# A copy moved to VectorE, four step orders, and the last feed-forward batches in banks of their own

## The reference, cut to what matters

```python
x = x + tanh(g_xattn[1]) * _L1_xattn_ref(_layernorm(x), ctx, ...)   # 16 heads of 16 channels, clipped scores
x = x + tanh(g_ffn[1])   * _L1_ffn_ref(_layernorm(x), ...)          # 16 heads, keys and values of one picked head
x = x + tanh(g_xattn[2]) * _L2_xattn_ref(_layernorm(x), ctx, ...)   # 16 heads of 128, 4 key heads, rotary, + context
x = x + tanh(g_ffn[2])   * _L2_ffn_ref(_layernorm(x), ...)          # 8-bit rows, ternary weights, hidden 1024
```

## Time and profile before

| | us |
|---|---|
| median of 3 runs | 2429.48 (2425.93 to 2430.18) |
| the profiled execution, own time | 2448.54 |
| its span, first to last instruction | 2446.4 |
| PE (TensorE matmuls) busy | 2169.1 (89%) |
| DVE (VectorE) busy | 1510.5 (62%) |
| ACT (ScalarE) busy | 1123.7 (46%) |
| POOL busy | 743.5 (30%) |

### The profile page before, as it was taken

One profiled execution on the slowest core, in us unless ns is written; L12 is line 12 of the kernel. 1 busy time (PEld: TensorE's weight loads), 2 busy tenths in 40 slices (PEclk: granted clock), 3 DMA queues, 4 the chain that ended last, 5 costly groups with the idle time before them and its releaser, 6 DMA issues. The chain is left out here.

```text
span 2446.4 us, 38415 instructions
## 1 busy us (share of the span) xinstructions
PE 2169.1 (89%) x10486; PEld 1377.7 (56%) x10486; DVE 1510.5 (62%) x3702; ACT 1123.7 (46%) x3555; POOL 743.5 (30%) x932
## 2 busy tenths in 40 slices
PE   6969999978799789978999999999998598979999
PEld 3446777855455344445555566566655355545685
DVE  6975434435566577765577677776776588843234
ACT  2022234411355355545555555556554288832242
POOL 5705510045333300013344444444443200003104
PEclk9969999989999899999999999999999599979999
DMA  6902245452400000000000000000000000201143
GB/s 217 310 17 84 92 131 162 155 156 81 172 1 0 3 1 0 0 26 1 1 1 1 0 0 0 0 0 0 0 0 1 4 6 5 107 3 46 63 136 97
DMA packets 85587, 127.18 MB, mean 52 GB/s; under 512 B 12418, under 2 KB 74626, under 8 KB 84226
## 3 DMA queue, kind: packets, MB, share of 16 engines
q1 hardware_dynamic: 75490, 98.52, 12.5%
q0 software_dynamic: 9984, 27.28, 3.5%
HBM read 91.41 MB, written 47.84 MB: 57 GB/s over the span
## 5 line engine op out<-in xcount | busy, mean ns | idle before, releaser
L2375 ACT ACTIVATE l2x_prob<-l2x_pS,l2x_nb,l2x_rms_q 128x256 f32<-128x256 f32 x256 | 142.5, 565 | 116.6 <-DVE l2x_nb L2610 114.8
L1035 ACT ACTIVATE moe_act_g<-moe_pG 128x96 f32<-128x96 f32 (+1 forms) x159 | 53.2, 335 | 279.3 <-PE moe_pU L968 119.8
L1186 PE MATMUL l2x_pQ<-big,l2x_xT 128*128 128x512 f32 x312 | 149.6, 602 | 4.8 <-DVE l2x_part L2588 4.3
L2607 DVE TENSOR_REDUCE l2x_negmax<-l2x_pS 128x2 f32<-128x512 f32 x128 | 87.8, 686 | 92.3 <-PE l2x_pS L2195 89.5
L928 POOL DMA_INDIRECT moe_yk<-route_y,moe_slot_i x72 | 69.6, 966 | 236.7 <-DMA route_y<-moe_y 187.5
L3117 DVE TENSOR_TENSOR l3f_hid<-l3f_act_g,l3f_pA 128x256 f32<-128x256 f32 (+1 forms) x103 | 38.1, 370 | 163.2 <-ACT l3f_act_g L3028 106.4
L2205 PE MATMUL l2x_pOT<-l2x_probT,l2x_v 128*128 128x512 f32 x256 | 124.7, 610 | 4.5 <-ACT l2x_probT L2390 4.5
L2195 PE MATMUL l2x_pS<-l2x_kT,l2x_qT 128*128 128x256 f32 x512 | 128.3, 380 | 0.0
L2941 PE MATMUL l3f_pA<-big,l3f_xnT 128*128 128x512 f32 x256 | 125.4, 614 | 0.0
L2214 PE MATMUL l2x_pT<-big,l2x_oT 128*128 128x256 f32 x512 | 121.1, 379 | 0.7 <-ACT l2x_oT L2383 0.7
L3028 ACT ACTIVATE l3f_act_g<-l3f_pA 128x256 f32<-128x256 f32 (+1 forms) x103 | 35.3, 343 | 183.4 <-PE l3f_pA L2941 183.4
(11 more groups left out here) (499 smaller groups left out, 5812.8 us busy)
## 6 DMA issues: line engine op xcount, KB each, us to landing
route_x<-in_c_zero SPq DMA_DIRECT2D x1, 13184.0 KB, 80.4
moe_xg<-route_x SPq DMA_DIRECT2D x103, 128.0 KB, 2.1
route_y<-moe_y SPq DMA_DIRECT2D x103, 128.0 KB, 1.7
big<-in_e_gu SPq DMA_DIRECT2D x1, 6144.0 KB, 19.2
l3f_xg<-route_x SPq DMA_DIRECT2D x39, 128.0 KB, 2.2
route_y<-l3f_y SPq DMA_DIRECT2D x39, 128.0 KB, 1.7
big<-in_f_gu SPq DMA_DIRECT2D x1, 4096.0 KB, 12.3
big<-in_e_down SPq DMA_DIRECT2D x1, 3072.0 KB, 25.2
```

What stands on the lines that cost most here:

```text
L1186: last = pe.matmul(out, lhsT=xT[:, k, :], rhs=w[:, k, cols], start=(k == 0), stop=(k == KC - 1))
L2375: ins = act.activation(prob[g % 2][:, h, :], pS[j][:, (h % 2) * 2 * P:(h % 2 + 1) * 2 * P], ACT.Exp, scale=rms_q[g][:, h:h + 1], bias=nb[: ...
L2607: dve.tensor_reduce(negmax[:, c], pS[j][:].rearrange("p (h k) -> p h k", h=2), AX.X, ALU.max, negate=True).then_inc(S["max_steps"], 1)
```

## The change

In `l1x` the whole copy of the turned keys is made by VectorE (`vector_whole`), the strips stay on ScalarE (`scalar_first`, `scalar_rest`). The step `turn` comes ahead of `normalise` and `zed`; `xT` moves behind `S3`, and `V2` ahead of `attT`, on TensorE and VectorE; ScalarE has `xT`, `attT`, `S3`. In `l1f` VectorE copies P2 ahead of the ternary step and the division, and ScalarE gets an order of its own, with P0's copy ahead of S1's exponential. In the rotary stage both `value_rows` move: for the batch's own rows into its slot 0, for the context into slot 1, each behind that slot's first `proj`. In slot 3 the output projection is cut in two halves of two heads, with the second transposes of probabilities between them. After the last slot `finish()` is written out by hand on each engine: batch 14's four projections go to `pQ`, `pTq`, `pS0`, `pS1`, and so do batch 15's, whose transposed row goes to `pP`; the hidden row of 14 is turned in `pOT`; batch 15 has a set of buffers of its own, laid over probabilities and queries that are no longer needed; the rounding of the hidden rows of 14 and 15 goes from POOL to ScalarE. The third narrow-head stage (`l3x`) is left as it is.

```diff
+    def vector_whole(self, dve, b, p):
+        dve.wait_ge(self.turned_ps, b + 1)
+        whole = self.ps_q[:, 0:4 * P] if self.spread == "k" else self.ps_k[:, 0:self.kt * P]
+        dve.tensor_copy(self.plain[p][:].rearrange("p m t -> p (m t)"), whole).then_inc(self.whole_read, 1)
+
+    def scalar_first(self, act, b, p):
+        act.wait_ge(self.turned_ps, b + 1)
+        if isinstance(b, int) and b == 0:
+            act.wait_ge(self.blank, 2)
+        parts = self.ps_k[:, 0:self.kt * P] if self.spread == "k" else self.ps_q[:, 0:4 * P]
+        self.strip(act, p, parts, 0)
+        self.strip(act, p, parts, 1)
...
-                      ("S1", 2), ("v", 1), ("V0", 2), ("rows", 1), ("S2", 2), ("normalise", 0), ("zed", 4),
-                      ("turn", 1), ("back", 3), ("divide", 3), ("V1", 2), ("spread", 1), ("xT", 0))
-        order = first_half + (("S3", 2), ("attT", 3), ("V2", 2))
-        act_order = first_half + (("attT", 3), ("S3", 2))
+                      ("S1", 2), ("v", 1), ("V0", 2), ("rows", 1), ("S2", 2), ("turn", 1), ("normalise", 0),
+                      ("zed", 4), ("back", 3), ("divide", 3), ("V1", 2), ("spread", 1))
+        order = first_half + (("S3", 2), ("xT", 0), ("V2", 2), ("attT", 3))
+        act_order = first_half + (("xT", 0), ("attT", 3), ("S3", 2))
...
+                after(pe, tq.whole_read, b)
+                    pe.wait_ge(tq.whole_read, b + 1)
...
-            steps = {"xT": lambda b, p: nm.scalar(act, b, p), "turn": lambda b, p: tq.scalar(act, b, p),
+            steps = {"xT": lambda b, p: nm.scalar(act, b, p), "turn": lambda b, p: tq.scalar_first(act, b, p),
-            pipeline(dve, order, steps, peel=6)
+            pipeline(dve, order, {**steps, "turn": lambda b, p: tq.vector_whole(dve, b, p)}, peel=6)
...
-        order = first_half + (("turn", 1), ("normalise", 0), ("S3", 2), ("ternary", 1), ("P2", 2), ("xT", 0),
-                              ("divide", 3))
+        order = first_half + (("normalise", 0), ("S3", 2), ("P2", 2), ("ternary", 1), ("divide", 3))
+        act_order = (("S0", 2), ("P3", 3), ("qkv", 1), ("P0", 2), ("S1", 2), ("oT", 3), ("S2", 2), ("turn", 1),
+                     ("S3", 2), ("xT", 0))
...
-            pipeline(act, order, {"xT": lambda b, p: nm.scalar(act, b, p), "qkv": gate, "turn": turn,
+            pipeline(act, act_order, {"xT": lambda b, p: nm.scalar(act, b, p), "qkv": gate, "turn": turn,
...
+        f_rows = (f_gate, f_val, f_th[:], f_xqT[:], f_qh_q[:], f_hqT)
+        f_rows_last = (prob[0][:].rearrange("p h k -> p (h k)"), prob[1][:].rearrange("p h k -> p (h k)"),
+                       probT[:].rearrange("p a h t -> p (a h t)"),
+                       qT[0][:, 0, :].bitcast(BF16).rearrange("p (k t) -> p k t", k=KC),
+                       krows[:].rearrange("p h d -> p (h d)").bitcast(BF16),
+                       qT[1][:].rearrange("p h t -> p (h t)").bitcast(BF16).rearrange("p (k t) -> p k t", k=HT))
+
+        def is_last(c, k=1):
+            return isinstance(c, int) and c >= B - k
+
+        def f_set(c):
+            return f_rows_last if is_last(c) else f_rows
+
+        def up_bank(c, n):
+            return (pQ, pTq, pS[0], pS[1])[n] if is_last(c, 2) else pF
+
+        def turn_bank(c, what):
+            return {("x", B - 1): pP, ("h", B - 2): pOT}.get((what, c), pF) if isinstance(c, int) else pF
...
-            def output(b, p, g):
+            def output_heads(g, hs):
+                for h in hs:
+                    last = pe.matmul(pT[:, C:2 * C], lhsT=oT[:, h, :], rhs=W["l2_wo"][:, 4 * g + h, :],
+                                     start=(h == 0), stop=(h == 3))
+                return last
+
+            def output_first(b, p, g):
                 pe.wait_ge(S["ot_read"], 4 * b + g + 1)
                 after(pe, S["added"], 4 * b + g)
-                for h in range(4):
-                    last = pe.matmul(pT[:, C:2 * C], lhsT=oT[:, h, :], rhs=W["l2_wo"][:, 4 * g + h, :],
-                                     start=(h == 0), stop=(h == 3))
-                last.then_inc(S["out_ps"], 1)
+                output_heads(g, (0, 1))
+
+            def output_second(b, p, g):
+                output_heads(g, (2, 3)).then_inc(S["out_ps"], 1)
+
+            def output(b, p, g):
+                output_first(b, p, g)
+                output_second(b, p, g)
...
+                if g < 2:
+                    value_rows(b, p, 1 - g)
                 if g == 3:
+                    output_first(*before(b, p, g, 2))
                     turn_probs(*before(b, p, g, 1), 1)
-                if at_least(b, g, 2):
+                    output_second(*before(b, p, g, 2))
...
-                if g == 0:
-                    value_rows(b, p, 0)
...
-                        value_rows(b + 1, 1 - p, 1)
...
             def finish():
+                f_up(B - 2, 0)
+                f_up(B - 2, 1)
                 turn_probs(B - 1, 1, 3, 0)
                 turn_probs(B - 1, 1, 3, 1)
                 output(B - 1, 1, 2)
                 values(B - 1, 1, 3, 2 * B)
+                f_up(B - 2, 2)
+                f_up(B - 2, 3)
                 output(B - 1, 1, 3)
-                for b in (B, B + 1):
-                    for g in range(4):
-                        f_first(b, g)
-                        f_second(b, g)
+                f_turn_h(B - 3)
+                f_out(B - 3)
+                f_turn_x(B - 1)
+                for n in range(4):
+                    f_up(B - 1, n)
+                f_turn_h(B - 2)
+                f_out(B - 2)
                 f_turn_h(B - 1)
                 f_out(B - 1)
...
+            def f_quant_h(c):
+                act.wait_ge(F["qh_steps"], 4 * c + 4)
+                if not is_last(c):
+                    act.wait_ge(F["hq_ps"], c)
+                act.activation(f_set(c)[4], f_set(c)[1], ACT.Copy, bias=-ROUND).then_inc(F["qh_ready"], 1)
...
                 values(B - 1, 1, 3)
-                for b in (B, B + 1):
-                    for g in range(4):
-                        f_middle(b, g)
-                        f_end(b, g)
+                f_tanh(B - 2, 0)
+                f_h_turned(B - 3)
+                f_tanh(B - 2, 1)
+                f_x_turned(B - 1)
+                f_quant_h(B - 2)
+                f_tanh(B - 1, 0)
+                f_h_turned(B - 2)
+                f_tanh(B - 1, 1)
+                f_quant_h(B - 1)
                 f_h_turned(B - 1)
...
+                f_quant_h(B - 3)
+                f_product(B - 2, 0)
+                fm.pool(pool, B - 1, 1)
+                f_product(B - 2, 1)
+                f_bias(B - 1)
+                f_product(B - 1, 0)
+                f_product(B - 1, 1)
...
                 add_out(B - 1, 1, 2)
+                f_evict(B - 2, 0, 0)
+                f_evict(B - 2, 0, 1)
                 add_out(B - 1, 1, 3)
-                for b in (B, B + 1):
-                    for g in range(4):
-                        f_first(b, b % 2, g)
-                        f_second(b, b % 2, g)
+                f_stats(B - 1, 1)
+                f_evict(B - 2, 0, 2)
+                f_evict(B - 2, 0, 3)
+                fm.normalise(dve, B - 1, 1)
+                f_quant_x(B - 1, 1)
+                f_hidden(B - 2, 0)
+                f_add(B - 3, 1)
+                f_hidden(B - 2, 1)
+                f_quant_h(B - 2, 0)
+                for n in range(4):
+                    f_evict(B - 1, 1, n)
+                f_hidden(B - 1, 0)
+                f_hidden(B - 1, 1)
+                f_quant_h(B - 1, 1)
+                f_add(B - 2, 0)
                 f_add(B - 1, 1)
```

78 lines of the change are left out of this document (45 added, 33 removed).

## The result

The changed kernel takes 2395.85 us (median of 4 runs, 2394.34 to 2396.73), the kernel before 2429.83 in its four runs beside it (one of them, at 3184.51, is in this median but left out of the ratio; without it the median is 2429.48): 0.9863, 95% interval 0.9851 to 0.9875, 34.0 us less. The prediction was 2394. The profiled execution took 2396.05 us, its span is 2394.0.

The account below looks back on a forecast made before the run. TensorE, 85 to 90% busy, bounds the three long windows, so only its idle time can go; the tail is a chain of handovers. 7.5 + 4.5 + 7.5 + 0 + 16 = 35.5 us off 2429.5 gives 2394, range 2374 to 2413.

Parts of the forecast that it names:

- Step 1: l1x: whole-key copy on VectorE lets the strips start 0.47 us earlier a turn, 7.5 us gained over 16 turns.
- Step 2: l1f: P2's copy ahead of the ternary steps, gain capped by the division, 0.3 us a turn, 4.5 us.
- Step 3: Rotary stage: value rows moved into slots 0 and 1, net 0.5 us a batch, 7.5 us gained.
- Step 4: Rotary slot 3: output projection split around the second transposes; idle time only moves before the product, gain 0 in the loop.
- The 0.65 us once in the last slot: Rotary stage's last slot: the split projection gains this once, as no squares stand ahead of ScalarE's copy.
- Step 5: End of the rotary stage: own banks and buffers for the last feed-forward batches, 15.8 us gained, called 16.
- the 15.2 worked out by that rule: Tail's saving in us if VectorE's two-operand SBUF instruction and a POOL instruction reading SBUF lock each other out.
- the carry from the profiled execution to the median: Whole kernel: the 35.5 us summed on the profiled execution (2448.54 us) was taken unchanged off the median, 2429.5.
- less: Rival: attention loops move by a third or less, the rotary loop by nothing; 19 us gained, 2410; chance 0.19.
- more: Rival: all targeted stalls go, including slot 3's ScalarE chain and more in l1f; 57 us gained, 2372; chance 0.11.
- the value-row copies on ScalarE: Rotary slots 0 and 1: two copies of 0.6 us hidden in ScalarE's idle time; slower rival had them exposed, chance 0.05.

Follow-up runs that it names:

- e10: The changed kernel without two of TensorE's waits on the whole-key copy in l1x's loop; a turn takes 11.27 us in place of 11.38.
- e8: The changed kernel with VectorE's division ahead of the ternary steps in l1f; a turn takes 13.60 us in place of 14.02, l1f 236.4 us.
- e7: The changed kernel with the context's value rows back at the end of slot 3; rotary batches take 48.30 and 49.5 us in turn, in place of 48.74.
- e9: The changed kernel with S2's exponential behind the strips and V2 behind the next first scores in l1x; turns of 11.49 and 11.8 us, l1x 209.6 us.
- d3: The kernel before with only the value rows moved into slots 0 and 1; the rotary stage gained 8.3 us, 48.75 us a batch.
- d1: The kernel before with only the whole-key copy on VectorE and l1x's orders and waits; l1x gained 8.6 us, the rotary stage took 4.0 us more.

## Why the prediction was right

**Step 1, `l1x`, 7.5 us predicted, 5.8 in the turns (0.36 x 16), 6.2 in the stage.** The mechanism is as drawn: the strips earlier by the copy, the division late but not last. The term was over by 0.11 us a turn, which is a wait added to TensorE's program; with it gone (e10) the turn is the 11.27 us of the prediction. The idle time left, 0.35 us, is less than the predicted 0.40 although the scores start later: TensorE's own steps between S2 and the scores, in their new order, take longer by 0.2 us (2.42 us in place of 2.2 from V1 to the end of the steps). So an idle time is a poor measure of what a turn gains; the chain's period is the measure.

**Step 2, `l1f`, 4.5 predicted, 3.5 in the stage with the part alone, 4.8 in the changed kernel.** With the part alone a turn is 0.30 us shorter, as drawn, and from the first such projection to the last the 15 turns give 4.5 us; the stage's end, behind the last projection, is 1.1 us longer (28.7 in place of 27.6), which the prediction had put at nothing. In the changed kernel a turn gains 0.24 us. The new wait before the projection is released by the division as predicted, at 0.49 us where 0.2 to 0.4 were given, and e8 shows that it was the cap. The 4.8 us hold an early turn that is 2.8 us shorter at the higher granted clock, which e7, e9 and e10 don't have with the same code, and a stage end that is 2.3 us longer, with 4 us at a granted clock of 0.57 in it.

**Step 3, value rows, 7.5 predicted, 8.3 in the stage, 0.54 us a batch where 0.5 was drawn.** The wait for the turned queries stands at 0.81 us where 0.8 to 1.0 was predicted, and e7 prices the cover that was given up at 0.44 us a batch.

**Step 4, the split, nothing predicted in the loop, nothing measured** (48.75 and 48.74 us). The idle time went from before the transposes to before the product, and the product waits for ScalarE's copy as read from the earlier trace rows. It went only half way, to 0.34 and 0.59 us. The 0.65 us once in the last slot are there: from the last transposes of the normalised rows to the last ones of probabilities it is 76.59 us in the kernel before, 77.72 with the value rows alone, 78.26 with the tail alone and 78.78 in the changed kernel, where the two increases together would make 79.39: 0.61 less.

**Step 5, the tail, 15.8 predicted, 14.9 in the changed kernel, 14.3 with the part alone.** By its terms: the last attention output was put 1.0 us later, with the 0.65 of the split already taken off; it is 1.06 later (1.67 with the tail alone, the split's 0.61 taken off), 0.96 of it a wait for ScalarE's copy of the input of the two projections ahead of the last transposes. The other two early projections cost nothing (6.79 us from those transposes to the last output, before and after). The move of the last rounding to ScalarE gave 1.70 (1.75). The term that was mis-sized is VectorE's run from the last attention output to the last rounding: 16.2 us drawn, 17.0 measured, so that it saved 14.3 us where 15.1 were counted. The whole window is 30.7 us, or 31.6 with the 0.9 us of the next stage that the earlier trace rows hold, where 31 to 33 were given, and VectorE's run has no gap of over 0.3 us; the hidden rows of the last batch fell on POOL's second product as feared. In the timeline, which shows that product and the first of the two VectorE instructions alone here, VectorE took 1.74 us where its second took 0.68:

```profile
1857.51 1.26 POOL L2573 TENSOR_TENSOR l2x_prob<-l2x_prob 128x512 f32<-128x512 f32 x1
...
1857.58 1.74 DVE L2759 SCALAR_TENSOR_TENSOR l2x_probT<-l2x_probT,l2x_prob 128x512 f32<-128x512 f32 x1
```

That instruction ran 1.06 us over its bare time. The Trainium skill (SBUF — State Buffer, Who interferes with whom) has such a pair lock each other out for a whole instruction; the trace agrees to about 0.1 us (a bare 0.68 behind POOL's end at 1858.77 would end at 1859.45, and it ended at 1859.32), and the time that the tail saved, 14.9 us, is nearer to the 15.2 worked out by that rule than to the 15.8 without it.

The sum: 6.2 + 4.8 + 22.5 = 33.5 of a predicted 35.5, and the carry from the profiled execution to the median held, since the 19 us between them lay in the experts' stage. That the sum came within 2 us is in part luck: the terms are off by -1.3, +0.3, +0.8 and -1.1 us (step 5 against its rounded 16), and against the parts alone the granted clock and the stage's end made `l1f` 1.4 us shorter and the first batch of the rotary stage 1.3 us longer (23.9 us in place of 22.6 in d3; from 16 to 20 us after the stage's start the clock is 0.66, and 1.00 in d3). Of the rivals, "less" was wrong about the rotary loop (it gained all of its 0.5 us), "more" about slot 3, and the value-row copies on ScalarE were hidden as said. What no part of the prediction saw is that ScalarE's gap could have taken back 4 us: in the changed kernel it is not at a place that counts, in d1 it is. As far as these runs show, that is an accident of the program's layout.

## What to carry to other kernels

Price a reordering by the period of the chain that sets the loop (here S0, S2, strips, S0), not by the idle time that it removes; and when an edit takes cover from a later wait, try putting half of it back. When one part of a change measures oddly in a stage that it doesn't touch, look for idle times with "issue" as the releaser that come once a loop turn (here 0.8 to 1 us behind the jump back), and shift the program by a few idle instructions before drawing a conclusion. Lay the granted clock of the first and last turns beside each other before a stage's length is credited to an edit. Waits that another wait on the same engine already covers are worth removing in a loop whose matmuls hang on a late release (0.11 us a turn for two of them here).
